# Turning the attention matrix of a two-layer graph network: from TensorE to VectorE blocks and DMAs

## The chip, the cores and the metric

The kernel runs on one core of a Trainium2 chip. The time is that of one execution on the device, in microseconds (us), from launch to end. Inputs lie in device memory.

## The reference, cut to what matters

64 graphs of 256 nodes with 512 features go through two layers. Each layer takes a normalised, rectified copy of x and adds its result to x.

```python
h = maximum(layernorm(x), 0)                    # layer 0: 4 heads of 64
q, k, v = heads(h @ Wq), heads(h @ Wk), heads(h @ Wv)
x = x + merge(softmax(where(adj, q k^T / 8, -max)) v) @ Wo + bo

h = maximum(layernorm(x), 0)                    # layer 1: 8 heads of 64
m = h @ map_w.T + map_b
cos = cosine(m, m) * ~adj                       # per head, 256 x 256
q, k = heads(m @ q_w.T + q_b), heads(m @ k_w.T + k_b)
p = softmax(where(adj, -1e10, q k^T / 8)) * keep
att = (cos > 0.1) * p                           # per head, 256 x 256
x = x + relu((att @ (h @ gcn_map_w.T + b)) @ gcn_W.T / (sum(att) + 1))
```

## The kernel before

One graph is one round. A round is software-pipelined: it runs the attention of layer 1 for graph a beside everything of graph n = a + 1 up to the layer-1 projections. There is a first round with no layer-1 attention, 62 rounds in a hardware loop, one more, and a last round with the attention of the last graph alone. The order of the work of each engine is written out by hand in five lists (L50 to L80: TENSOR, SCALAR, VECTOR, POOL, SYNC); each engine walks its own list strictly in order, and semaphores join them. A name in quotes (`"qk0"`, `"vv0"`) is a step of graph n, a pair (`("cos", 2)`) one of graph a for the head pair 2 of 0 to 3. Where two steps of one engine stand in the list, the second never starts before the first.

Layer-1 attention, for each pair p of heads a and b:

- `score` (L800, helper L767): TensorE makes q k^T into two PSUM banks, one for each head; VectorE (`score_a`, `score_b`, L607) masks it into the SBUF tile `att` and finds the row's extreme; ScalarE (`exp_a`, `exp_b`, L475) takes the exponential in place.
- `cos` (L804): TensorE makes the cosines into two more banks; VectorE (`cos_a`, `cos_b`, L618) compares them with 0.1 and multiplies `att` in place.
- `turn_a`, `turn_b` (L808, helper L743): TensorE transposes `att` of one head, four blocks of 128 x 128, into the head's score bank, and ScalarE (L481) copies it to the SBUF tile `uT`. There is one `uT`, with room for one pair.
- `value` (L812, helper L779): TensorE multiplies v by `uT` (8 matmul records of 256 columns for the pair); ScalarE copies the result (L485), `back` on TensorE turns it (L817), on VectorE scales it (L634), on GpSimd adds it to `x_res` (L410).

`att` has two buffers, used by pairs alternately. Of layer 0 and the projections, `ht` are transposes of h, `qk`, `m`, `q`, `k`, `v0`, `vv`, `wo` are projections (L755, L763), `s` scores, `pt` transposes of the probabilities, `av` their product with v, `ss`, `rt`, `bc` the norms for the cosines. In the TENSOR list `value` 3 is followed by `vv0`, `ss`, all `q` and `k` projections and `vv1` of graph n, and only then comes `score` 0 of the next round.

The DMAs of the loop are issued by SyncE (its queue is SP in the profile), four for each graph: the next x, the result, a copy of `x_mid` to `x_res`, the next adjacency matrix. Each names all 128 partitions.

Of the kernel before, what the change touches and what calls it, by code (L numbers as in the profile page):

```python
# [18 lines left out]
COS_THRESHOLD = 0.1  # L19
MASKED_L1 = -1e10  # L20
# [3 lines left out]
def gnn_two_layers(nc, x, adj, wq, wk, wv, wo, bo, map_t, map_b, q_t, q_b, k_t, k_b, gcn_map, gcn_map_b, gcn_t, out):  # L24
# [26 lines left out]
        "ht0a", ("score", 0), "ht0b", ("cos", 0), "qk0", "qk1", ("turn_a", 0), "qk2", ("turn_b", 0), "s0", "s1", ("value", 0),  # L51
        "qk3", ("back", 0), ("score", 1), ("cos", 1), "s2", "s3", "pt0", "v0", "pt1", ("turn_a", 1), ("turn_b", 1), "pt2",
        "pt3", ("value", 1), "av", ("back", 1), ("score", 2), ("cos", 2), "wo0", "wo1", ("turn_a", 2), ("turn_b", 2),
        ("value", 2), ("score", 3), ("back", 2), "ht1a", "ht1b", ("cos", 3), "m0", "m1", "m2", ("turn_a", 3), ("turn_b", 3),
# [17 lines left out]
    ]  # L72
    POOL = [
        ("unit", 0), "mid", "mask0", "sum0", "sum1", ("unit", 1), ("back", 0), "sum2", "sum3", "rstd1", ("back", 1),
        ("back", 2), "m0", "rstd0", "m1", "m2", "m3", "pow", "mask1", ("back", 3)
    ]
# [5 lines left out]
    bank_of = {s: 4 + k % PBANKS for k, s in enumerate(PRODUCTS)}  # L82
# [21 lines left out]
    with ctx:  # L104
# [40 lines left out]
        att = sb("att", [128, 2, 2, C, N])  # L145
# [5 lines left out]
        gcn_rows = att[:, :, :, :, :].rearrange("p a b c n -> p (a b c n)").rearrange("p (h d) -> p h d", d=D)  # L151
# [77 lines left out]
        gram_full = count("gram_full")  # L229
        gated = count("gated")  # L230
        t_full = count("t_full")
        uT_ready = count("uT_ready")
        uv_full = count("uv_full")
        oT1_ready = count("oT1_ready")
        o_full = count("o_full")
# [692 lines left out]
```

## Time and profile before

| | |
|---|---|
| runs | 4121.55 us median of 3 (4118.8 to 4130.23) |
| the profiled execution | 4121.26 us, span 4119.5 us |
| mean granted TensorE clock | 0.993 |
| TensorE busy | 3931.4 us, 95% |
| VectorE busy | 2608.3 us, 63% |
| ScalarE busy | 1979.3 us, 48% |
| GpSimd busy | 1324.3 us, 32% |

The page gives the busy time of each engine, then the span in 40 slices with tenths of busy time in each. The slices are even from the second to the last but one: the rounds are alike, so one round of the timeline stands for all. A matmul's recorded time holds its latency, and neighbours overlap; what one costs in a dense stream is read from start to start.

### The profile page before, as it was taken

To read this page: it belongs to the slowest core of one execution; us is meant where nothing else is said; L and a number is where in the kernel's file an instruction comes from. 1 tells how busy PE (TensorE), PEld (TensorE's weight loads), DVE (VectorE), ACT (ScalarE), POOL (GpSimd) and SP (SyncE) were. 2 spreads that over 40 slices of the span, in tenths; PEclk is the share of its full clock that TensorE was granted. 3 is DMA by queue.
4 is the path that set the end of the run, shared out by engine and by line. 5 is a ranking of instruction groups with operands and counts; after the bars stand their busy time and mean duration, and the time that the engine had idled before them with its cause. 6 is when DMAs were issued, how large, how long until landed. Compare 5 with 4: busy or idle time off the path is not lost.

```text
span 4119.5 us, 105002 instructions
## 1 busy us (share of the span) xinstructions
PE 3931.4 (95%) x32976; PEld 3437.0 (83%) x32976; DVE 2608.3 (63%) x9426; ACT 1979.3 (48%) x5583; POOL 1324.3 (32%) x2007
## 2 busy tenths in 40 slices
PE   7999999999999999999999999999999999999997
PEld 6888888888888888888888888888888888888886
DVE  4666666666666666666666666666666666666664
ACT  3554544544545445445454454454454544544544
POOL 3333333333332333333333333333333333333332
PEclk8999999999999999999999999999999999999998
DMA  3000000000000000000000000000000000000000
GB/s 87 16 32 26 22 32 16 32 32 16 32 27 21 32 18 30 32 16 32 29 18 32 22 25 32 16 32 32 16 32 27 21 32 16 32 32 16 32 27 17
DMA packets 65544, 111.77 MB, mean 27 GB/s; under 512 B 20880, under 2 KB 22448, under 8 KB 65520
## 3 DMA queue, kind: packets, MB, share of 16 engines
q1 hardware_dynamic: 64928, 110.12, 7.8%
q0 software_dynamic: 592, 1.35, 0.2%
q8 instruction: 13, 0.21, 0.0%
q14 instruction: 11, 0.09, 0.0%
HBM read 44.34 MB, written 33.55 MB: 19 GB/s over the span
## 4 chain that ended last, share of the span: by engine, by line
PE 65%; DVE 12%; issue 11%; ACT 6%; POOL 4%; DVEq 1%; DMA 1%; POOLq 0%; ACTq 0%; SPq 0%
PE bank L755 34%; PE bank L763 9%; PE bank L748 7%; PE bank L783 6%; PE bank L775 4%; ACT prob L501 3%; PE bank L883 3%; POOL prob L417 2%; DVE x_mid L663 2%; ACT att L475 2%; DVE prob L650 2%; DVE att L607 2%; DVE att L618 1%; POOL rstd L362 1%; DVE hT L640 1%
## 5 line engine op out<-in xcount | busy, mean ns | idle before, releaser
L475 ACT ACTIVATE att<-att,nmax 128x256 f32<-128x256 f32 x1024 | 509.7, 500 | 299.6 <-DVE nmax L607 299.6
L417 POOL TENSOR_SCALAR prob<-prob,rsum 128x256 f32<-128x256 f32 x512 | 241.1, 487 | 631.2 <-DVE rsum L657 628.2
L755 PE MATMUL bank<-hT,w_qkv 128*128 128x256 f32 x3072 | 414.9, 288 | 4.7 <-DVE hT L640 4.7
L755 PE MATMUL bank<-qkm,w_k 128*128 128x256 f32 x3072 | 416.6, 285 | 0.0
L755 PEld LDWEIGHTS bank<-hT,w_qkv 128*128 128x128 f32 x3072 | 376.9, 189 | 37.9 <-issue 24.2
L755 PE MATMUL bank<-hT,w_map 128*128 128x256 f32 x3072 | 396.7, 285 | 5.1 <-DVE hT L640 1.0
L618 DVE SCALAR_TENSOR_TENSOR att<-bank,att 128x256 f32<-128x256 f32 x1024 | 392.3, 420 | 4.0
L755 PE MATMUL bank<-qkm,w_q 128*128 128x256 f32 x3072 | 390.8, 283 | 0.0
L755 PEld LDWEIGHTS bank<-hT,w_map 128*128 128x128 f32 x3072 | 372.5, 189 | 18.4 <-DVE hT L640 17.3
L763 PE MATMUL bank<-w_v,hT 128*128 128x512 f32 x1536 | 385.3, 399 | 0.0
L755 PEld LDWEIGHTS bank<-qkm,w_k 128*128 128x128 f32 x3072 | 380.1, 188 | 5.0
L481 ACT ACTIVATE uT<-bank 128x512 f32<-128x512 f32 x512 | 292.2, 598 | 181.1 <-PE bank L748 169.5
L515 ACT ACTIVATE q<-bank,bias_q 128x256 fp32r<-128x256 f32 x256 | 121.0, 473 | 537.1 <-PE bank L755 535.2
L607 DVE CUSTOM_DVE_ANT_0 att<-bank,mask 128x256 f32<-128x256 f32 x1024 | 372.1, 420 | 7.3 <-PE bank L775 2.3
L755 PEld LDWEIGHTS bank<-qkm,w_q 128*128 128x128 f32 x3072 | 373.4, 189 | 0.1
L763 PEld LDWEIGHTS bank<-w_v,hT 128*128 128x128 f32 x1536 | 278.6, 188 | 82.6 <-issue 24.2
L783 PE MATMUL bank<-uT,v 128*64 128x256 f32 x2048 | 280.1, 395 | 49.4 <-ACT uT L481 49.4
L410 POOL TENSOR_TENSOR x_res<-x_res,rel 128x256 f32<-128x256 f32 x256 | 189.0, 738 | 420.4 <-DVE rel L634 420.4
L689 DVE SCALAR_TENSOR_TENSOR q<-bank,bias_q,q 128x256 fp32r<-128x256 f32 x256 | 117.1, 478 | 321.4 <-ACT q L515 321.4
L359 POOL TENSOR_SCALAR var_e<-mv 128x2 f32<-128x2 f32 x128 | 24.7, 193 | 913.9 <-DVE mv L540 913.9
L634 DVE SCALAR_TENSOR_TENSOR rel<-bank,fac 128x256 f32<-128x256 f32 x256 | 108.7, 424 | 314.6 <-PE bank L820 310.1
L515 ACT ACTIVATE k<-bank,bias_k 128x256 fp32r<-128x256 f32 x256 | 121.5, 474 | 373.9 <-PE bank L755 373.9
(122 smaller groups left out, 7949.6 us busy)
## 6 DMA issues: line engine op xcount, KB each, us to landing
x_in<-x SPq DMA_DIRECT2D x64, 512.0 KB, 3.4
x_res<-x_mid SPq DMA_DIRECT2D x64, 512.0 KB, 3.1
out<-x_res SPq DMA_DIRECT2D x64, 512.0 KB, 2.8
adj<-adj SPq DMA_DIRECT2D x64, 64.0 KB, 2.6
att<-gcn_map POOLq DMA_DIRECT2D x2, 512.0 KB, 9.0
x_mid<-wq SPq DMA_DIRECT2D x1, 512.0 KB, 5.6
x_res<-wk SPq DMA_DIRECT2D x1, 512.0 KB, 6.8
v<-wv SPq DMA_DIRECT2D x1, 512.0 KB, 7.7
```

What stands on the lines that cost most here:

```text
L410: g.tensor_tensor(part, part, rel[:, :, :], ALU.add).then_inc(res_added, 1)
L417: last = g.tensor_scalar(prob0[:, hd, c, :], prob0[:, hd, c, :], rsum0[:, hd, c:c + 1], 0.0, ALU.mult, ALU.add)
L475: s_.activation(e_sl, e_sl, ACT.Exp, bias=nmax1[:, p, c, e:e + 1], scale=-1.0, accum_out=esum1[:, p, c, e:e + 1]).then_inc(exp1_done, 1)
L481: s_.activation(uT[:, e, :], t_bank[e][:, :], ACT.Copy).then_inc(uT_ready, 1)
L515: s_.activation(dst[:, 0, t, :], bank[bank_of[kind]][:, 0:N], ACT.Identity, bias=bias[:, t:t + 1]).then_inc(high_done, 1)
L607: v_.tensor_tensor_reduce(out=att[:, p % 2, e, c, :], in0=score_bank[e][:, c * N:c * N + N], in1=mask1[:, c, :], scale=-SCALE, scalar=FLT_ ...
L618: v_.scalar_tensor_tensor(e_sl, gram_bank[e][:, c * N:c * N + N], COS_THRESHOLD, e_sl, ALU.is_gt, ALU.mult, accum_out=usum1[:, p, c, e:e + ...
L748: last = t_.transpose(dst[:, b * 128:b * 128 + 128], src_of(outer, c), ident[:, :])
L755: last = t_.matmul(dst, w(ws, k)[:, t * 128:t * 128 + 128], rhs[:, rs, k, :], start=(k == 0 and i == 0), stop=(k == KT - 1 and i == 2))
L763: last = t_.matmul(dst, lhs[:, ls, k, c * 128:c * 128 + 128], w(ws, k), start=(k == 0 and i == 0), stop=(k == chunks - 1 and i == 2))
L775: last[e] = t_.matmul(banks[e][:, c * N:c * N + N], left[r, ls, c * 128:c * 128 + 128], right[r, rs, :], start=(i == 0), stop=(i == 2))
L783: last = t_.matmul(dst[64 * e:64 * e + 64, :], v[:, jc, (hd0 + e) * DH:(hd0 + e + 1) * DH], rhs(e, jc), start=(jc == 0), stop=(jc == C - 1))
```

## The change

- `turn_a` and `turn_b` go from TensorE and from ScalarE. VectorE gets `flip_a` and `flip_b` instead: one instruction for each head transposes every 32 x 32 block of `att` (128 partitions x 512 elements) in place.
- SyncE gets a step `("shift", p)` for each pair: it waits until `value` of the pair before is done (`uv_full`, since `uT` still has one buffer), and then, for each head, waits for the head's flip and issues 16 DMAs. Each carries 32 partitions x 128 elements (512 bytes a partition, 16 KB in all) from `att` to `uT`, so that the blocks come to lie where the whole transpose has them. `value` p waits for all 32 DMAs of its pair.
- The tile `att` is laid out in blocks. `score` and `cos` on TensorE read their right side and write PSUM in pieces of 32 elements; `value` reads `uT` so; the mask of layer 1 is made in that order too.
- `value` and `back` share PSUM bank 4; the other products of graph n have three banks in place of four. `score` and `cos` wait for VectorE's reads of their banks.
- All five lists are put in a new order.

```diff
     TENSOR = [
...
+        ("score", 0), "ht0a", "ht0b", ("cos", 0), ("score", 1), "qk0", "qk1", "qk2", "qk3", "s0", "s1", ("cos", 1),
+        ("score", 2), "s2", "s3", ("value", 0), "v0", "pt0", "pt1", ("back", 0), "pt2", "pt3", ("cos", 2), "av", ("value", 1),
+        ("score", 3), "wo0", "wo1", ("back", 1), ("cos", 3), ("value", 2), "ht1a", "ht1b", ("back", 2), "m0", "m1", "m2", "m3",
+        ("value", 3), "vv0", "ss", ("back", 3), "q0", "k0", "q3", "rt", "k3", "q2", "bc0", "q1", "k1", "k2", "vv1", "bc1"
     ]
     SCALAR = [
...
+        ("unit", 0), "ht0a", "ht0b", ("exp_a", 0), ("exp_b", 0), "qk0", "qk1", ("unit", 1), ("exp_a", 1), "qk2", "qk3",
+        ("exp_b", 1), "exp0", "exp1", ("value", 0), "exp2", "exp3", "pt0", "pt1", "pt2", "pt3", ("exp_a", 2), ("exp_b", 2),
+        "av", ("exp_a", 3), ("exp_b", 3), ("value", 1), ("value", 2), "ht1a", "ht1b", "m0", "m1", "m2", "m3", ("value", 3),
+        "q0", "k0", "q3", "k3", "q2", "q1", "k2", "k1"
     ]
     VECTOR = [
...
+        ("score_a", 0), ("score_b", 0), "ht0a", "ht0b", ("cos_a", 0), ("flip_a", 0), ("cos_b", 0), "qk0", ("flip_b", 0),
+        ("score_a", 1), "qk1", "qk2", ("score_b", 1), ("factor", 0), "qk3", "s0", ("cos_a", 1), "s1", "sum0", "s2", "s3",
+        ("flip_a", 1), "sum1", ("cos_b", 1), "sum2", ("flip_b", 1), "sum3", "v0", ("back", 0), ("factor", 1), ("score_a", 2),
+        ("score_b", 2), ("cos_a", 2), ("cos_b", 2), ("flip_a", 2), ("factor", 2), "av", ("flip_b", 2), ("score_a", 3),
+        ("score_b", 3), "wo0", "wo1", ("back", 1), ("cos_a", 3), "norm1", ("flip_a", 3), ("cos_b", 3), "ht1a", "ht1b",
+        ("flip_b", 3), "m0", "m1", ("back", 2), ("factor", 3), "stats0", "m2", "m3", "vv0", ("back", 3), "ss", "norm0", "q0",
+        "k0", "q3", "rt", "k3", "q2", "bc0", "q1", "k1", "k2", "vv1", "bc1"
     ]
     POOL = [
...
+        "mask0", ("unit", 0), "mid", ("unit", 1), "sum0", "sum1", "sum2", "sum3", ("back", 0), "rstd1", ("back", 1), "m0",
+        "m1", ("back", 2), "mask1", "rstd0", "m2", "m3", "pow", ("back", 3)
     ]
-    PBANKS = 4
+    PBANKS = 3
     SYNC = [
-        "x", ("out", 0), "move", "adj"
+        ("shift", 0), ("shift", 1), ("shift", 2), "x", ("shift", 3), ("out", 0), "adj", "move"
     ]
...
-        att = sb("att", [128, 2, 2, C, N])
+        att = sb("att", [128, 2, 4, 2, C, C, 32])
...
+                    elif kind == "shift":
+
+                        sp.wait_ge(uv_full, pairs(a, p))
+                        sp.sem_inc(passed_sync, 1)
+                        for e in range(2):
+                            sp.wait_ge(flipped, pairs(a, p, 2) + e + 1)
+                            sp.sem_inc(passed_sync, 1)
+                            for rows in range(4):
+                                for cols in range(4):
+                                    sp.dma_start(uT_blocks[32 * cols:32 * cols + 32, rows, e, :, :, :].rearrange("p c j f -> p (c j f)"),
+                                                 att[32 * rows:32 * rows + 32, p % 2, cols, e, :, :, :].rearrange("p c j f -> p (c j f)")).then_inc(turned[p], 16)
...
-                    elif kind in ("turn_a", "turn_b"):
-                        e = "ab".index(kind[5])
-                        act.wait_ge(t_full, pairs(a, p, 2) + e + 1)
-                        act.wait_ge(uv_full, pairs(a, p))
-                        s_.activation(uT[:, e, :], t_bank[e][:, :], ACT.Copy).then_inc(uT_ready, 1)
...
+                        if e == 0:
+                            dve.wait_ge(turned[(p + 2) % 4], BLOCK_MOVES * (a + (1 if p < 2 else 2)))
+                            dve.sem_inc(passed_vector, 1)
...
+                    elif kind in ("flip_a", "flip_b"):
+
+                        e = "ab".index(kind[5])
+                        dve.wait_ge(gated, pairs(a, p, 4) + 2 * e + 2)
+                        dve.sem_inc(passed_vector, 1)
+                        blocks = att[:, p % 2, :, e, :, :, :].rearrange("p b c j f -> p b (c j f)")
+                        v_.transpose(blocks, blocks).then_inc(flipped, 1)
...
+                    elif kind == "value":
+                        pe.wait_ge(turned[p], BLOCK_MOVES * (a + 2))
                         pe.wait_ge(rel_done, pairs(a, p))
-                    elif kind in ("turn_a", "turn_b"):
-                        e = "ab".index(kind[5])
-                        pe.wait_ge(gated, pairs(a, p, 4) + 2 * e + 2)
-                        transposes(t_bank[e], lambda jc, c: att[:, p % 2, e, c, jc * 128:jc * 128 + 128]).then_inc(t_full, 1)
```

## Rows read from the trace of the kernel before

**Rows 1.** Busy time of each engine in one round (--windows, steady state), clock and DMA last.

```profile
core 0: us, PE busy (x) PEld busy (x) DVE busy (x) ACT busy (x) POOL busy (x), PEclk, DMA share, GB/s
2000.00:2063.15 63.15, 60.91 (x516) 53.31 (x514) 40.53 (x147) 30.70 (x87) 20.52 (x31) 1.00 0.08 26
```

**Rows 2.** Waits of the whole span: who waited for whom, us in total, times, longest.

```profile
SPq L309 <- POOL x_res L410: 3414.3, 64, 62.2
```

**Rows 3.** Timeline of SyncE's queue: start, duration of the issue, in steady rounds.

```profile
2048.52 0.40 SPq L310 DMA_DIRECT2D out<-x_res  x1
2051.41 0.47 SPq L321 DMA_DIRECT2D x_res<-x_mid  x1
2111.69 0.40 SPq L310 DMA_DIRECT2D out<-x_res  x1
```

**Rows 4.** The same view at the kernel's start: DMAs issued back to back.

```profile
0.75 0.45 SPq L285 DMA_DIRECT2D x_in<-x  x1
1.26 0.45 SPq L286 DMA_DIRECT2D adj<-adj  x1
1.75 0.47 SPq L294 DMA_DIRECT2D x_mid<-wq  x1
2.27 0.51 SPq L294 DMA_DIRECT2D x_res<-wk  x1
2.81 0.51 SPq L294 DMA_DIRECT2D v<-wv  x1
```

**Rows 5.** Four lines' issues: count, ns min/median/max, first and last start us.

```profile
L305 SPq DMA_DIRECT2D x_in<-x x63: 368/387/397, 35.2 to 3952.0; - x63
L310 SPq DMA_DIRECT2D out<-x_res x64: 394/396/411, 154.0 to 4115.0; - x64
L321 SPq DMA_DIRECT2D x_res<-x_mid x64: 472/480/537, 56.4 to 4075.5; - x64
L326 SPq DMA_DIRECT2D adj<-adj x63: 373/392/400, 84.1 to 4009.7; - x63
```

**Rows 6.** From issue to landing, us: first of L321, then of L326.

```profile
DMA to landing us min/median/max: 2.9/3.1/3.1
...
DMA to landing us min/median/max: 1.8/2.6/4.3
```

**Rows 7.** Timeline of TensorE in one round: value 3 to score 0.

```profile
2032.91 1.08 PE L783 MATMUL bank<-uT,v 128*64 128x256 f32 x8
2033.92 3.06 PE L763 MATMUL bank<-w_v,hT 128*128 128x512 f32 x12
2053.80 0.60 PE L748 MATMUL bank<-ident,h 128*128 128x128 f32 x4
2054.33 0.97 PE L775 MATMUL bank<-k,q 64*128 64x256 f32 x12
```

**Rows 8.** Timelines: last cos_a 0 of that round; score 0, turn of the last round.

```profile
2058.88 0.42 DVE L618 SCALAR_TENSOR_TENSOR att<-bank,att 128x256 f32<-128x256 f32 x1
...
4077.93 0.98 PE L775 MATMUL bank<-k,q 64*128 64x256 f32 x12
4081.34 0.65 PE L748 MATMUL bank<-ident,att 128*128 128x128 f32 x4 [1.38 <-DVE att L618]
```

**Rows 9.** VectorE groups by line: busy us, mean ns of one, idle before.

```profile
L549 DVE CAST pick<-uT 128x512 fp32r<-128x512 f32 x1 | 0.4, 426 | 4.0 <-POOL uT L350 4.0
L546 DVE TENSOR_SCALAR h<-x_mid,mv,rstd 128x512 f32<-128x512 f32 x128 | 89.2, 736 | 84.3 <-POOL rstd L362 84.3
```

**Rows 10.** Windows while TensorE stands, and while it is busy again.

```profile
56.00:58.00 2.00, 0.00 (x0) 0.00 (x0) 1.24 (x4) 0.00 (x0) 0.29 (x2) 1.00 0.20 80
60.00:62.00 2.00, 1.68 (x8) 1.68 (x8) 0.26 (x1) 0.00 (x0) 0.00 (x0) 0.55 0.00 0
36.00:38.00 2.00, 2.00 (x14) 2.00 (x12) 1.19 (x7) 0.38 (x1) 0.00 (x0) 0.50 0.93 353
42.00:43.00 1.00, 1.00 (x6) 1.00 (x6) 0.00 (x0) 0.47 (x1) 0.00 (x0) 0.50 0.00 0
43.00:44.00 1.00, 1.00 (x9) 1.00 (x9) 0.00 (x0) 0.00 (x0) 0.00 (x0) 0.94 0.00 0
```

**Rows 11.** Timeline of TensorE in the last round: a value at the lower clock.

```profile
4101.00 1.97 PE L783 MATMUL bank<-uT,v 128*64 128x256 f32 x8 [0.69 <-ACT uT L481]
```

**Rows 12.** Timeline of TensorE: two turns of att and what follows.

```profile
2071.98 1.04 PE L748 MATMUL bank<-ident,att 128*128 128x128 f32 x8
2072.86 1.34 PE L748 MATMUL bank<-ident,prob 128*128 128x128 f32 x8
```

**Rows 13.** TensorE's wait for uT, in the waits; packets of SyncE's queue.

```profile
PE bank L783 <- ACT uT L481: 49.4, 67, 0.8
...
q1 hardware_dynamic: 64928, 110.12, 7.8%
```

More of the change, by code:

```diff
@@ L50, in gnn_two_layers @@
     TENSOR = [
[L51 to L54, printed above, removed]
@@ L75, in gnn_two_layers @@
-        ("back", 2), "m0", "rstd0", "m1", "m2", "m3", "pow", "mask1", ("back", 3)
+        "mask0", ("unit", 0), "mid", ("unit", 1), "sum0", "sum1", "sum2", "sum3", ("back", 0), "rstd1", ("back", 1), "m0",
+        "m1", ("back", 2), "mask1", "rstd0", "m2", "m3", "pow", ("back", 3)
     ]
-    PBANKS = 4
+    PBANKS = 3
     SYNC = [
-        "x", ("out", 0), "move", "adj"
+        ("shift", 0), ("shift", 1), ("shift", 2), "x", ("shift", 3), ("out", 0), "adj", "move"
     ]
     PRODUCTS = [s for s in TENSOR if isinstance(s, str)]
-    bank_of = {s: 4 + k % PBANKS for k, s in enumerate(PRODUCTS)}
+    bank_of = {s: 5 + k % PBANKS for k, s in enumerate(PRODUCTS)}
@@ L230, in gnn_two_layers @@
         gated = count("gated")
-        t_full = count("t_full")
-        uT_ready = count("uT_ready")
+        flipped = count("flipped")
+        turned = [count(f"turned{p}") for p in range(PAIRS1)]
         uv_full = count("uv_full")
@@ L286, in _ @@
                 sp.dma_start(adj8[:, :, :], adj[0].rearrange("(c p) j -> p c j", p=128)).then_inc(adj_loaded, 16)
+                for p in range(PAIRS1):
+                    sp.sem_inc(turned[p], BLOCK_MOVES)
                 for k, (src, _) in enumerate(PIECES):
@@ L430, in body @@
                             pool.sem_inc(passed_gpsimd, 1)
-                        g.tensor_scalar(mask1[:, :, :], adj8[:, :, :], MASKED_L1, 0.0, ALU.mult, ALU.add).then_inc(mask1_ready, 1)
+                        for c in range(C):
+                            g.tensor_scalar(mask1[:, c, :].rearrange("p (b j f) -> p b j f", j=C, f=32),
+                                            adj8[:, c, :].rearrange("p (j b f) -> p b j f", j=C, f=32), MASKED_L1, 0.0,
+                                            ALU.mult, ALU.add).then_inc(mask1_ready, 1)
                         for c in range(C):
@@ L601, in body @@
                             if p == 0:
[L602 to L605 removed]
+                                dve.wait_ge(mask1_ready, C * (a + 1))
+                        if e == 0:
+                            dve.wait_ge(turned[(p + 2) % 4], BLOCK_MOVES * (a + (1 if p < 2 else 2)))
+                            dve.sem_inc(passed_vector, 1)
                         for c in range(C):
[L607 removed]
+                            v_.tensor_tensor_reduce(out=att[:, p % 2, :, e, c, :, :].rearrange("p b j f -> p b (j f)"), in0=in_blocks(score_bank[e][:, c * N:c * N + N]), in1=in_blocks(mask1[:, c, :]),
                                                     scale=-SCALE, scalar=FLT_MAX, op0=ALU.add, op1=ALU.min,
@@ L765, in project_rows, with by_quarter, head_products @@
                 return last
-            def head_products(banks, left, right):
+            def by_quarter(ap, source):
+                return ap.rearrange("p (j b f) -> p b j f", j=C, f=32) if source else ap.rearrange("p (b j f) -> p b j f", j=C, f=32)
+            def head_products(banks, left, right, order=lambda ap, source: ap):
                 last = [None, None]
@@ L774, in head_products @@
                             r = slice(64 * e, 64 * e + 64)
-                            last[e] = t_.matmul(banks[e][:, c * N:c * N + N], left[r, ls, c * 128:c * 128 + 128], right[r, rs, :],
-                                                start=(i == 0), stop=(i == 2))
+                            last[e] = t_.matmul(order(banks[e][:, c * N:c * N + N], False), left[r, ls, c * 128:c * 128 + 128],
+                                                order(right[r, rs, :], True), start=(i == 0), stop=(i == 2))
                 return last
@@ L782, in values @@
                     for e in range(2):
-                        last = t_.matmul(dst[64 * e:64 * e + 64, :], v[:, jc, (hd0 + e) * DH:(hd0 + e + 1) * DH], rhs(e, jc),
+                        last = t_.matmul(dst[64 * e:64 * e + 64, :].rearrange("p (c r f) -> p c r f", c=C, f=32), v[:, jc, (hd0 + e) * DH:(hd0 + e + 1) * DH], rhs(e, jc),
                                          start=(jc == 0), stop=(jc == C - 1))
@@ L856, in body @@
                         for t in range(PAIRS0):
-                            last = values(full[:, t * N:t * N + N], v0, 2 * t, lambda e, jc: ptm[:, 2 * t + e, jc * N:jc * N + N])
+                            last = values(full[:, t * N:t * N + N], v0, 2 * t, lambda e, jc: ptm[:, 2 * t + e, jc * N:jc * N + N].rearrange("p (c r f) -> p c r f", c=C, f=32))
                         last.then_inc(product_full, 1)
```

45 lines of the change are left out of this document (16 added, 29 removed), and 3 rows, old and new, of the table VECTOR.

## The prediction

> **What bounds the kernel now.** I read the page's busy times first, then one round by windows, then the timelines of TensorE and of SyncE's queue. One round, from one result's store to the next, takes 2111.69 - 2048.52 = 63.2 us [rows 3]; 64 of them are the kernel. In a round TensorE is busy 60.9 us at the full clock, VectorE 40.5, ScalarE 30.7 [rows 1]. So TensorE's own stream is the round, and whatever leaves it would shorten it. SyncE's queue does next to nothing: it waits 3414 us of the span for the add that completes a result [rows 2], and issues four DMAs a round.
>
> **What leaves TensorE.** The turns of a pair take 2072.86 - 2071.98 = 0.88 us from start to start [rows 12], 3.5 us a round for four pairs. TensorE's wait for `uT`, 49.4 us in all, is 0.8 us a round [rows 13]. Were nothing late in their place, a round would take 63.2 - 4.3 = 58.9 us. ScalarE loses eight copies; it isn't the bound and this is worth nothing.
>
> **What is put in their place is a chain of its own.** `uT` has one buffer. The shift of pair p waits for `value` p-1, `value` p waits for the shift's 32 DMAs, and TensorE takes both in order. So from one `value` to the next there lie: the end of `value`, a hop to SyncE, 32 issues one after the other, the landing of the last, and nothing can overlap them but TensorE's other work. The question is what one issue costs.
>
> *One issue, T.* SyncE's rows show no 16 KB DMA, so I bound it. An issue takes the same for 64 KB (392 ns median, adjacency) as for 512 KB (387 ns, x) [rows 5]: its price doesn't follow the bytes, and I don't expect a small one to be cheaper. The cheapest of either is 368 ns; with the gap of 0.04 to 0.06 us to the next issue [rows 4], T is at least 0.42. The only copy from SBUF to SBUF, which these are, takes 480 ns [rows 5]: 0.53 with the gap. DMAs issued back to back start 0.49 to 0.54 us apart [rows 4], though none of them is from SBUF; with the 0.09 that SBUF to SBUF takes more, 0.63 is the upper end. I take 0.53, where two rows meet, and keep 0.42 and 0.63.
>
> The Trainium skill's page "DMA: Bandwidth & Descriptors", in its section on why a DMA increments its semaphore by 16, gives 512 sequencer cycles for a copy instruction on chips before the accelerated path; at the 1.2 GHz that "Trainium Kernel Development and Optimization" (NeuronCore Architecture) gives SyncE that is an estimate of 0.43 us. The rows' 0.37 to 0.51 lie about it; by it the round would come out near my cheap end.
>
> *Landing, L, from the last issue's start.* 2.6 us median for 64 KB, as little as 1.8; 3.1 for 512 KB from SBUF to SBUF [rows 6]. I take 2.4, nearer to the smaller transfer, with 1.8 and 3.1 as ends.
>
> *Hop.* The add into `x_res` ends 0.2 us before the store is issued; I take 0.2 for semaphore hops, an estimate that 0.1 either way moves by 0.8 us in two hops a pair.
>
> *Value.* 1.08 us at the full clock [rows 7], 1.97 at half [rows 11].
>
> *The first shift's chain:* 31 x 0.53 + 2.4 + 0.2 = 19.0 us from flip a of pair 0 to `value` 0. Flip b comes some 2 us behind flip a, within the 16 x 0.53 = 8.5 us that head a's issues take, so it costs nothing; beginning with the first head saves just that.
>
> *From value to value:* 1.97 + 19.0 = 21.0 us, three times: 63.0. Beside it TensorE has only v0, four pt, back, cos and av (about 8 us), then score 3, two wo, cos 3 (about 8), then two ht1 and four m (about 8): it stands for over half the time. VectorE's and ScalarE's work for the next pair fits in the same 21 us, so its flips are not late. The wait of `score_a` 2 for pair 0's DMAs is passed already when `value` 0 has run.
>
> *From value 3 to flip a 0 of the next round.* This stretch has no shift to hide in or beside, as `value` 3 stands ahead of vv0, ss, all q and k and vv1, and score 0 behind them. The old round takes 2054.33 - 2032.91 = 21.4 us from `value` 3 to score 0, with ht0a (2054.33 - 2053.80 = 0.5) between, which now comes later: 20.9 [rows 7]. From score 0 to the end of cos_a is 5.0 us in the full round (2059.30 less 2054.33) [rows 7, 8] and 3.4 in the last, where no ht stands between [rows 8]; with both ht behind score 0, I take 4.2. The flip of 128 x 512 is bounded by VectorE's other instructions of that size, 0.43 to 0.74 [rows 9]; no row shows a transpose on it. I take the dearer: 0.7. Together 4.9, ends 3.8 and 5.7. Seven of the eight flips, some 5 us, lie beside SyncE's issues; VectorE at 46 us is far from a bound here.
>
> SyncE's other work lies in that stretch too: out, adj and move, with the wait for the store to land (2051.41 - 2048.52 = 2.9 us [rows 3]), are some 14 us behind `value` 3, before the flip at 26. The load of x stands between shift 2 and shift 3: 0.39 us [rows 5], and while `value` 2 is awaited, so nothing.
>
> *TensorE's clock.* It stands 10 to 12 us ahead of each `value`. After the stop at 56 us the clock was at 1.00 for a while and at 0.55 in the window from 60; with TensorE fully busy from 36 us on, it stayed 0.50 up to 43 us and was 0.94 in the next [rows 10]: 1.2 GHz for 8 us of work, then 2.4. I expect this behind every stop. It costs three values 0.9 each (2.7, the fourth is within the next term) and the stretch behind `value` 3 the half of 8 us, 4.0. The other work beside the shifts has room.
>
> *The sum.* 20.9 + 4.0 + 4.9 + 19.0 + 63.0 = 111.8 us a round. With 64 rounds: the first result is stored at 154 us in this trace and the last 4.5 us before the end [rows 5], so 91 us of start stand ahead of the first round; in the last one nothing is queued between `value` 3 and the store, which I estimate at 9.5 us less. 91 - 9.5 + 4.5 = 86; 64 x 111.8 + 86 = 7241, and 2 us around the span (4121.26 to 4119.5; the median is 4121.55, the same). **7240 us.** The start's own new order and the three PSUM banks I put at nothing: TensorE waits more than it works. If pieces of 32 elements slow matmuls, score 0 and four values show it: doubled, 0.9 + 4 x 1.1 = 5.3 us a round, 340 us, within the range.
>
> **The rivals.**
>
> *A. Issues at their cheap end.* T 0.42, L 1.8: shift chain 15.0, round 20.9 + 4.9 + 15.0 + 3 x 16.1 = 89.0 with the clock kept, 5,780 us; with it lost 95.7, 6,210. For it: 368 to 392 ns are most of the loop's rows. Against: the one SBUF to SBUF row.
>
> *B. T 0.53, and the clock holds.* 105.1 a round, 6,810 us. Stops of 4 us have left it at 1.00 [rows 10]; these are longer.
>
> *C. Issues at their dear end.* T 0.63, L 3.1: shift chain 22.8, round 24.9 + 5.7 + 22.8 + 3 x 24.8 = 127.7, 8,260 us.
>
> *D. Not slower: a small DMA is issued nearly for nothing, and the transfers set the shift.* SyncE's packets took 0.078 x 4119.5 x 16 / 64,928 = 0.079 us each [rows 13]. A pair has 1,024, 64 on each engine: 5.1 us. Then the shift chain is 7.7, the round 20.9 + 4.9 + 7.7 + 3 x 8.8 = 59.9, just above TensorE's 58.9: 4121 - 63 x 3.3 = 3,910 us. It holds as long as 124T + 39.4 is under 63.2: T under 0.19. Against it stand all rows of the queue, the lowest at 0.37. The time from 0.19 to 0.42 would be slower already.
>
> The Trainium skill speaks for D: "DMA: Bandwidth & Descriptors", section "Issuing engines are not separate DMA queues", says the sequencer's time to initiate a DMA is usually small beside the DMA. In the rows 0.4 of 3 us is small indeed; but here 32 of them are in series behind one wait and the landing is paid once, so I give that rule little.
>
> **How the numbers follow.** My forecast 45%, A 24%, B 10%, C 15%, D and all else that ends at or below today's time 6%. The range is 5,750 to 8,000: it takes in A and B and most of the way to C. About 0.3% is what a measurement of this kernel can tell from no change (12 us). Slower 0.94, same 0.01, faster 0.05.
>
> **What would show it.** In the changed kernel's timeline SyncE's queue has runs of 32 issues with starts 0.53 us apart, 128 a round; the waits put TensorE's `value` behind these DMAs, near 45 us a round; the page has TensorE under 60% busy and a mean clock well under 0.99. The round is 112 us from store to store. Wrong would be: issues under 0.2 us apart (D); `value` waiting for anything else; or starts at 0.53 us and a round far from 105 to 112, which would mean that the chain isn't serial as the code reads.

## The result, and the profile after

The changed kernel takes 7836.5 us (median of 4 runs, 7835.3 to 7838.4) where the kernel before takes 4121.9: a ratio of 1.901, 95% interval 1.897 to 1.904. It is slower, by 3715 us. The forecast was 7240 us, with a range of 5750 to 8000.

The page of the changed kernel: busy time of the engines, the granted clock by slices (tenths of full speed), and the chain that ended last by line.

```profile
span 7834.8 us, 109125 instructions
...
PE 4256.1 (54%) x30928; PEld 3595.7 (46%) x30928; DVE 2998.1 (38%) x9938; ACT 1722.7 (22%) x5071; POOL 1352.6 (17%) x2071
...
PEclk7777777777777777777777777777777777777776
...
SPq L321 59%; PE bank L777 9%; PE bank L809 7%; DMA uT<-att 6%; PE bank L785 6%; PE bank L906 1%; PE bank L770 1%; PE bank L801 1%; DVE hT L663 1%; DVE att L642 1%; DVE att L634 1%; DVE att L623 0%; PE bank L918 0%; PE bank L843 0%; SPq L317 0%
```

Before, the chain that ended last lay 65% on TensorE; now 59% of it is L321, SyncE issuing the moves from `att` to `uT`. No engine is busy for more than 54% of the span.

One round, store to store, by windows; it answers to [rows 1].

```profile
3958.51:4079.18 120.67, 65.69 (x484) 55.59 (x483) 46.55 (x155) 26.69 (x79) 20.97 (x32) 0.76 0.11 31
```

120.7 us in place of 63.2. TensorE is busy for 65.7 us of it, where it was 60.9, with a mean granted clock of 0.76; what is new is 55 us in which it stands. This round is a little shorter than most: from the first store to the last (201.5 to 7831.7 us, 63 steps) the mean is 121.1. SyncE's queue in the same stretch, which answers to [rows 3]:

```profile
3974.18 67.72 SPq L321 DMA_DIRECT2D uT<-att  x96
4042.36 0.40 SPq L311 DMA_DIRECT2D x_in<-x  x1
4045.35 20.21 SPq L321 DMA_DIRECT2D uT<-att  x32
4079.18 0.41 SPq L327 DMA_DIRECT2D out<-x_res  x1
4082.22 0.54 SPq L338 DMA_DIRECT2D x_res<-x_mid  x1
4094.85 35.19 SPq L321 DMA_DIRECT2D uT<-att  x50
```

32 issues of a pair last 20.2 us; the 96 of three pairs, with the two waits between them, 67.7. TensorE's side, its timeline at values 2 and 3 (last column: idle before, and who ended it):

```profile
4043.13 1.97 PE L809 MATMUL bank<-uT,v 128*64 128x256 f32 x8 [14.69 <-DMA uT<-att]
...
4066.83 1.98 PE L809 MATMUL bank<-uT,v 128*64 128x256 f32 x8 [13.31 <-DMA uT<-att]
```

From value 2 to value 3 it is 23.7 us: 1.97 of value and 0.25 to the first issue (4045.35), 19.6 to the last issue, 1.8 to its landing. `value` waits for the DMAs 256 times, once a pair and graph, 3518 us in all:

```profile
PE bank L809 <- DMA uT<-att: 3518.3, 256, 20.8
```

And the line of the moves and the flips, in ns min/median/max and by form (busy us, mean ns):

```profile
L321 SPq DMA_DIRECT2D uT<-att x8192: 507/590/1357, 95.4 to 7825.4; - x200
...
DMA to landing us min/median/max: 1.7/1.8/3.0
...
L642 DVE STREAM_TRANSPOSE att<-att 128x512 f32<-128x512 f32 x512 | 361.0, 705 | 10.7 <-DVE att L634 9.6
```

### The profile page after: what moved, and what is told of

Same layout as the page of the kernel before. It is cut to its first block, busy times and chain, and to the rows that moved or that the text cites. A ratio compares the mean times of both kernels' runs of the same rounds, so it can differ in the third digit from the quotient of the medians.

```text
span 7834.8 us, 109125 instructions
## 1 busy us (share of the span) xinstructions
PE 4256.1 (54%) x30928; PEld 3595.7 (46%) x30928; DVE 2998.1 (38%) x9938; ACT 1722.7 (22%) x5071; POOL 1352.6 (17%) x2071
## 3 DMA queue, kind: packets, MB, share of 16 engines
q0 software_dynamic: 592, 1.35, 0.1%
## 4 chain that ended last, share of the span: by engine, by line
SPq 60%; PE 26%; DMA 6%; issue 6%; DVE 3%; DVEq 0%; POOL 0%; ACT 0%; POOLq 0%; ACTq 0%
SPq L321 59%; PE bank L777 9%; PE bank L809 7%; DMA uT<-att 6%; PE bank L785 6%; PE bank L906 1%; PE bank L770 1%; PE bank L801 1%; DVE hT L663 1%; DVE att L642 1%; DVE att L634 1%; DVE att L623 0%; PE bank L918 0%; PE bank L843 0%; SPq L317 0%
## 5 line engine op out<-in xcount | busy, mean ns | idle before, releaser
L809 PE MATMUL bank<-uT,v 128*64 128x256 f32 x2048 | 505.4, 647 | 3518.3 <-DMA uT<-att 3518.3
L809 PEld LDWEIGHTS bank<-uT,v 128*64 128x64 f32 x2048 | 196.3, 217 | 3684.3 <-DMA uT<-att 3587.0
L499 ACT ACTIVATE oT<-bank 128x256 f32<-128x256 f32 x256 | 97.4, 380 | 3115.9 <-PE bank L809 3115.9
L663 DVE SCALAR_TENSOR_TENSOR hT<-bank,hT 128x512 fp32r<-128x512 f32 x256 | 167.9, 686 | 887.2 <-ACT hT L503 871.8
L708 DVE TENSOR_TENSOR v<-bank,bias_v 128x512 f32<-128x512 f32 x128 | 88.6, 692 | 1085.8 <-PE bank L785 1085.8
L785 PE MATMUL bank<-w_v,hT 128*128 128x512 f32 x1536 | 460.3, 457 | 0.0
L461 POOL TENSOR_TENSOR rn<-ssq,minus_half 128x16 f32<-128x16 f32 x64 | 200.4, 3131 | 1136.3 <-DVE ssq L715 1136.3
L785 PEld LDWEIGHTS bank<-w_v,hT 128*128 128x128 f32 x1536 | 335.8, 227 | 123.4 <-issue 47.7
L680 DVE RECIPROCAL rsum<-esum 128x2 f32<-128x2 f32 x256 | 39.4, 154 | 919.5 <-ACT prob L515 919.2
L441 POOL TENSOR_TENSOR ptm<-ptm 128x256 f32<-128x256 f32 x256 | 154.9, 617 | 1330.8 <-DVE qkm L694 1330.8
```

Of the source, the lines that this page charges most:

```text
L441: g.tensor_tensor(msq[:, t, :], m32[:, t, :], m32[:, t, :], ALU.mult).then_inc(msq_done, 1)
L461: g.tensor_tensor(rn[:, :], ssq[:, :], minus_half[:, :], ALU.pow).then_inc(rn_done, 1)
L499: s_.activation(oT1[:, :], v_bank[0][:, 0:N], ACT.Copy).then_inc(oT1_ready, 1)
L663: v_.scalar_tensor_tensor(flat(hT[:, 1, t:t + 2, :]), full[:, :], 0.0, flat(hT[:, 0, t:t + 2, :]).bitcast(F32), ALU.max, ALU.subtract).the ...
L785: last = t_.matmul(dst, lhs[:, ls, k, c * 128:c * 128 + 128], w(ws, k), start=(k == 0 and i == 0), stop=(k == chunks - 1 and i == 2))
L809: last = t_.matmul(dst[64 * e:64 * e + 64, :].rearrange("p (c r f) -> p c r f", c=C, f=32), v[:, jc, (hd0 + e) * DH:(hd0 + e + 1) * DH], r ...
```

## The experiments

The theory behind the forecast: the loss is a serial chain, 32 issues and one landing for each pair, between two values that share one `uT`. The rivals are that the landings, the bytes, the new order or the clock make it. Numbers 2 to 7 and 9 are single runs; where a time is said to change there, it changes by over 3%, and the runs of one kernel here differ by 0.3%.

**1. One DMA for each head.** The rest of the change stays, so this is what the change costs without its moves.

```diff
-                            for rows in range(4):
-                                for cols in range(4):
+                            for rows in range(1):
+                                for cols in range(1):
```

> One DMA for each head in place of 16; the other 15 are left out, so most of uT is not written. Theory (the 32 issues in series between two values are the loss, 0.65 us each as the changed kernel's trace has them): a chain shrinks by 30 issues, 19.5 us, and TensorE's own stream is the round again, 59 to 61 us, 3,830 to 3,950 us in all, faster than before. Rival 1 (the new order, the three banks, the block layout and the flips cost much by themselves): a round over 63.2 us, 4,150 us or more. Rival 2 (the landing of a DMA, not its issue, is the loss): hardly less than 7,800 us.

4001.3 us (3999.2 to 4002.3), ratio to before 0.970 (0.969 to 0.972): faster than the kernel before. A round, from one adjacency load to the next (2046.11 to 2107.87), is 61.8 us. TensorE's three largest waits:

```profile
PE bank L770 <- DVE h L561: 77.2, 64, 8.3
PE bank L809 <- DVE rel L657: 54.0, 63, 0.9
PE bank L785 <- DVE oT L682: 30.7, 63, 0.5
```

No wait for a DMA is among them. So 30 issues a pair are worth 3835 us, with the clock's fall in the waits for them, and what is left of the change (turns gone, order, banks, blocks, flips) is a gain of 3%. It lies outside the 3,830 to 3,950 us that I expected: a round gains 1.4 us and not the 4.3 that I had counted for TensorE's turns and its wait for `uT`. All waits of TensorE but that for `uT` are 123 us in the kernel before and 224 here, 1.6 us a round more, and the mean clock is 0.977 in place of 0.993. Here the clock falls behind two stops, ahead of `value` 2 and ahead of `ht1a`, with 1.1 us of work between them, as the 1.87 us of the second row show. The kernel before has stops of 0.74 and 1.35 us in the same stretch, with 2.4 us of work between them, and its clock holds (third and fourth rows):

```profile
2084.94 1.08 PE L809 MATMUL bank<-uT,v 128*64 128x256 f32 x8 [0.84 <-DVE rel L657]
2087.11 1.87 PE L770 MATMUL bank<-ident,h 128*128 128x128 f32 x8 [1.09 <-DVE h L561]
...
2083.55 1.08 PE L783 MATMUL bank<-uT,v 128*64 128x256 f32 x8 [0.74 <-ACT uT L481]
...
2087.26 1.09 PE L748 MATMUL bank<-ident,h 128*128 128x128 f32 x8 [1.35 <-DVE h L546]
```

Score and value take 0.98 and 1.08 us at the full clock, as before: reading in pieces of 32 elements costs TensorE nothing that shows.

**2. The same DMAs with half the bytes.** 256 bytes a partition; half of `uT` isn't written.

```diff
-uT_blocks[32 * cols:32 * cols + 32, rows, e, :, :, :] ... att[..., cols, e, :, :, :]
+uT_blocks[32 * cols:32 * cols + 32, rows, e, 0:1, :, :] ... att[..., cols, e, 0:1, :, :]
```

> All 32 DMAs of a pair, each with 256 bytes a partition in place of 512; half of uT is not written. Theory (an issue's price doesn't follow the bytes): starts stay 0.65 us apart, 7,800 us. Rival (the queue is held up by what the DMA engines still have to move, which is why 0.65 stands where 0.53 was forecast): starts at 0.53 us or less, 120.7 - 124 x 0.12 = 106 us a round, 6,870 us or less.

7836.1 us, no change, and the same duration of an issue:

```profile
L321 SPq DMA_DIRECT2D uT<-att x8192: 507/590/1272, 95.1 to 7824.8; - x200
```

From 512 to 256 bytes a partition, bytes play no part, neither in the issue nor in a queue of work behind it.

**3. One DMA for both heads.** 16 for a pair, 1024 bytes a partition, after flip b.

```diff
-                        for e in range(2):
-                            sp.wait_ge(flipped, pairs(a, p, 2) + e + 1)
+                        sp.wait_ge(flipped, pairs(a, p, 2) + 2)
...
-att[32 * rows:32 * rows + 32, p % 2, cols, e, :, :, :]
+att[32 * rows:32 * rows + 32, p % 2, cols, :, :, :, :]
```

> The two heads of a pair go in one DMA: 16 for a pair with 1024 bytes a partition, begun when both heads are flipped; nothing is left out. Theory (price by the count of issues): value to value falls from 23.7 by 16 x 0.65 = 10.4 to 13.3 us, the round from 120.7 by 41.6 to 79 us plus some 2 us for waiting for flip b of pair 0, 81 us, 5,270 us. Rival (price by bytes): 7,800 us.

5751.5 us. The count sets the price: 16 issues are 10.0 us. But a round is 88.8 us (2030.39 to 2119.14 between two stores), not 81. The timelines of SyncE and TensorE:

```profile
2094.28 10.03 SPq L320 DMA_DIRECT2D uT<-att  x16
...
2088.32 1.98 PE L808 MATMUL bank<-uT,v 128*64 128x256 f32 x8 [4.72 <-DMA uT<-att]
2105.63 1.97 PE L808 MATMUL bank<-uT,v 128*64 128x256 f32 x8 [6.18 <-DMA uT<-att]
```

Value 2 is over at 2090.3, the shift of pair 3 begins at 2094.3, as flip b comes only then. With 32 issues there was room for it; with 16 the flips are the late ones at two of the three shifts behind a value, which my expectation had only for pair 0.

**4. Two issuing engines.** Head b's 16 DMAs are ScalarE's, four at a time between its other steps.

```diff
+                    elif kind[:5] == "shift":
+                        rows = int(kind[5])
+                        if rows == 0:
+                            act.wait_ge(uv_full, pairs(a, p))
+                            act.wait_ge(flipped, pairs(a, p, 2) + 2)
+                        for cols in range(4):
+                            act.dma_start(uT_blocks[..., rows, 1, ...], att[..., cols, 1, ...]).then_inc(turned[p], 16)
```

> Head a's 16 DMAs issued by SyncE, head b's 16 by ScalarE, in four groups between its other steps; nothing is left out. Theory (each issuing engine pays its own 0.65 us): value to value falls by up to 10.4 us, to 14 to 16 us as ScalarE has other steps between, the round to 80 to 90 us, 5,200 to 5,850 us. Rival (both queues share what generates the descriptors): starts twice as far apart while both issue, 7,500 us or more.

6185.5 us, a round of 95.6: a gain, and less than expected. Each engine pays its own price, hardly more beside the other's:

```profile
L322 SPq DMA_DIRECT2D uT<-att x4096: 507/592/1524, 93.6 to 6173.9; - x196
...
L503 ACTq DMA_DIRECT2D uT<-att x4096: 513/612/1811, 95.2 to 6174.2; - x196
```

The rival of a shared generator falls. What is short of the expectation is no longer the DMAs alone: TensorE waits 573 us for them, but 372 and 182 us for ScalarE's copies (`oT`, `ptm`), which now stand behind its issues, and 395 and 210 us for VectorE. One pair's ScalarE issues ran from 2025.7 to 2036.1 us, and its value at 2040.8, 19.0 us behind the value before it in place of 14 to 16, waited for no DMA: TensorE had stood 2.9 us for ScalarE's copy of `ptm` just ahead of `av`.

**5. TensorE kept busy in its waits.**

```diff
+                        pe.wait_ge(rel_done, pairs(a, p))
+                        for _ in range(100):
+                            t_.matmul(bank[4][:, N:2 * N], w_k[:, 0, 0, 0:128], w_k[:, 0, 1, 0:N], start=True, stop=True)
                         pe.wait_ge(turned[p], BLOCK_MOVES * (a + 2))
-                        pe.wait_ge(rel_done, pairs(a, p))
```

> TensorE is given 100 matmuls of 256 columns (12 us at the full clock) ahead of each value, into the unused half of bank 4, whose result nobody reads, in the time in which it waits for the DMAs. Theory (the clock's fall is a term of its own: the values behind a stop at half the clock, and the first work behind each): value takes 1.08 in place of 1.97 us, the stretch behind value 3 is some 4 us shorter, the round 120.7 - 6.7 = 114 us, 7,410 us in all, at a mean clock near 1. Rival (TensorE's clock is hidden by the chain, as the chain waits for nothing of TensorE but value): 7,830 less 64 x 0.9 x 4, 7,600 us; or, if the matmuls run longer than the wait, above 7,830 us.

7583.6 us, mean clock 0.972 in place of 0.752: 253 us less, 4.0 a round. The direction is right and the size nearer to the rival. Timelines of TensorE and SyncE:

```profile
2048.24 12.14 PE L837 MATMUL bank<-w_k 128*128 128x256 f32 x100
2061.36 1.08 PE L809 MATMUL bank<-uT,v 128*64 128x256 f32 x8 [0.98 <-DMA uT<-att]
...
2087.83 32.35 SPq L321 DMA_DIRECT2D uT<-att  x47
```

Value is back at 1.08 us (three of them count, 2.7; the fourth lies in the stretch behind value 3), and from value 3 to the next shift it is 26.5 us, where the changed kernel has 4094.85 - 4066.83 = 28.0: 1.5 and not 4.0. In the changed kernel the clock behind value 3 is back sooner than [rows 10] had it:

```profile
4069.00:4070.00 1.00, 1.00 (x3) 0.81 (x4) 0.00 (x0) 0.24 (x1) 0.00 (x0) 0.50 0.00 0
4070.00:4071.00 1.00, 1.00 (x5) 0.77 (x5) 0.00 (x0) 0.00 (x0) 0.00 (x0) 0.90 0.00 0
```

A mean of 0.90 in the second window puts the return at about 4070.2, 3.4 us behind the start of value 3; what half the clock cost in that time is half of it, 1.7.

**6. The price of an issue by itself.** The kernel before, with six groups of eight DMAs on SyncE's idle queue in each round.

```diff
+                    elif kind == "probe":
+                        for i in range(8):
+                            sp.dma_start(probe[32 * (i % 4):32 * (i % 4) + 32, ...], bias_v[...]).then_inc(probed, 16)
+                        sp.wait_ge(probed, 768 * a + 128)
...
```

> The kernel before with a step on SyncE's idle queue in each round: six groups of eight DMAs into a tile that nothing reads, each group waited for: 32 partitions x 512 bytes from SBUF; the same with 128 bytes; with 1024 bytes; 128 partitions x 256 bytes from SBUF; 32 partitions x 512 bytes from device memory; 16 partitions x 512 bytes from SBUF. Theory (SBUF to SBUF and back to back each add to an issue, bytes and partitions don't): 0.65 us apart for every group from SBUF, 0.05 to 0.1 less from device memory. Rival (the price follows the descriptors): 16 partitions half of 32, 128 partitions four times. The time stays within 1% of 4,120 us, as the queue has 57 us idle a round and nothing waits for it but the store of the result, or rises where that store comes late.

4124.3 us, unchanged. The six groups by line: 32 partitions x 512 bytes; x 128; x 1024; 128 partitions x 256 bytes; from device memory; 16 partitions x 512 bytes.

```profile
L312 SPq DMA_DIRECT2D probe<-bias_v x512: 521/590/995, 101.3 to 4082.7; - x171
L316 SPq DMA_DIRECT2D probe<-bias_v x512: 507/591/1425, 107.6 to 4088.9; - x171
L320 SPq DMA_DIRECT2D probe<-bias_v x512: 507/591/1319, 114.6 to 4095.1; - x171
L324 SPq DMA_DIRECT2D probe<-bias_v x512: 465/602/678, 120.9 to 4104.3; - x171
L328 SPq DMA_DIRECT2D probe<-wq x512: 331/421/1326, 127.4 to 4109.4; - x171
L332 SPq DMA_DIRECT2D probe<-bias_v x512: 561/589/818, 132.3 to 4115.5; - x171
```

From SBUF to SBUF an issue is 0.59 to 0.60 us whatever its bytes and its partitions; from device memory 0.42. The rival by descriptors falls. Eight from SBUF last 4.94 us, so their starts are (4.94 - 0.59) / 7 = 0.62 us apart; the pair's 32 are (20.21 - 0.59) / 31 = 0.63. Eight from device memory last 3.60 us, 0.45 apart. That back to back costs something too shows where the trace of the changed kernel is cut to the beginning of the shift at 4045.35: the first issue takes 0.52 us, the ones behind it 0.59, with 0.04 of gap.

**7. Two buffers for `uT`.** A shift waits for the value two pairs before. For the room the two masks are in bfloat16.

```diff
+        uT_odd = sb("uT_odd", [128, 2, C * N])
...
-                        sp.wait_ge(uv_full, pairs(a, p))
+                        sp.wait_ge(uv_full, pairs(a, p) - 1)
```

> uT has two buffers, by pair, and a shift waits for value of the pair two before it; for the room both masks are in bfloat16 (with 3e38 for the largest float). All 32 DMAs of a pair stay. Theory (the chain is issue, landing, hop and value in series; with two buffers the issues of four pairs run on one after the other, and landing, hop and value fall out three times; what stays in series is the 26 us from value 3 to the next flip a): 26 + 4 x 20.8 + 2 = 111 us a round, 7,230 us. Rival 1 (the queue alone is the bound): 128 x 0.65 + 2 = 85 us, 5,550 us. Rival 2 (no change, as the single buffer isn't what holds the shifts): 7,830 us.

7290.4 us, a round of 112.6 (1997.76 to 2110.39 between two stores). SyncE's queue:

```profile
1997.76 0.41 SPq L328 DMA_DIRECT2D out<-x_res  x1
...
2013.44 20.23 SPq L322 DMA_DIRECT2D uT<-att  x32
2034.06 20.21 SPq L322 DMA_DIRECT2D uT_odd<-att  x32
2054.58 20.18 SPq L322 DMA_DIRECT2D uT<-att  x32
...
2075.94 20.21 SPq L322 DMA_DIRECT2D uT_odd<-att  x32
```

The shifts run on with 0.3 to 0.4 us between them, 1.2 at the last, where the load of x stands; the round is 1.6 us over the 111 expected. The single buffer costs 8 us a round of the 57 lost. The four shifts take 83 of the 112.6, and the stretch behind value 3 still stands in series with them.

**8. Value one stage later.** 16 DMAs a pair (as 3), two buffers (as 7), and new lists in which value p stands behind work that hides the moves. Nothing is left out.

```diff
-        ("score", 2), "s2", "s3", ("value", 0), "v0", "pt0", "pt1", ("back", 0), "pt2", "pt3", ("cos", 2), "av", ("value", 1),
...
+        "s1", ("cos", 1), "s2", ("score", 2), "s3", "v0", "pt0", "pt1", "pt2", "pt3",
+        ("cos", 2), "av", ("value", 0), ("score", 3), "wo0", "wo1", ("back", 0), ("cos", 3), ("value", 1), "ht1a",
+        "ht1b", ("back", 1), "m0", "m1", "m2", "m3", ("value", 2), ("back", 2), "q0", "ss",
...
```

> The whole computation: 16 DMAs for a pair with 1024 bytes a partition, uT in two buffers, masks in bfloat16, and all five lists in another order, in which value p stands one stage later (value 0 behind av, value 1 behind wo, value 2 behind m, value 3 among the q and k projections, ahead of vv0). Theory (the DMAs cost only while TensorE waits for them; a pair now takes 15 x 0.63 + 1.8 = 11.3 us from flip b to value, and SyncE's 64 issues 41 us of a round): TensorE's own stream is the round, as it was with one DMA for each head, 61 to 62.5 us, 3,950 to 4,040 us, 2 to 4% faster than before. Rival (issues that run beside other DMAs, or the flips' and the waits' places, still hold value up): over 63.2 us a round, above 4,120 us.

4162.6 us, ratio 1.010 (1.008 to 1.011): slower than the kernel before by 1.0%. TensorE waits for DMAs 30.5 us in all, but once a round for VectorE's `back` 0 (143.4 us), with the clock falling behind it:

```profile
2032.47 1.08 PE L813 MATMUL bank<-uT_odd,v 128*64 128x256 f32 x8 [2.16 <-DVE rel L661]
...
2032.00:2040.00 8.00, 7.02 (x45) 6.11 (x46) 6.34 (x19) 3.87 (x13) 1.05 (x2) 0.79 0.34 109
```

The moves are nearly hidden, and the theory failed all the same: TensorE's own stream is not the round. The rival has the number right, and of its two causes the one that shows is a wait's place; a delay by DMAs beside other DMAs does not.

**9. The same without the new order.** Against number 8:

```diff
-        "s1", ("cos", 1), "s2", ("score", 2), "s3", "v0", "pt0", "pt1", "pt2", "pt3",
-        ("cos", 2), "av", ("value", 0), ("score", 3), "wo0", "wo1", ("back", 0), ("cos", 3), ("value", 1), "ht1a", ...
+        ("score", 2), "s2", "s3", ("value", 0), "v0", "pt0", "pt1", ("back", 0), "pt2", "pt3", ("cos", 2), "av", ("value", 1),
+        ("score", 3), "wo0", "wo1", ("back", 1), ("cos", 3), ("value", 2), "ht1a", "ht1b", ("back", 2), ...
```

> The same 16 DMAs for a pair, the same two buffers and masks, in the order of the changed kernel. Theory: what is left of the chain is flip b to value 11.3 us a pair, in part beside the issues of the next; value p stands ahead of the work that could hide it, and the scores of pair 2 stand behind back 0 on VectorE, so values alternate with waits: 79 to 86 us a round, 5,150 to 5,600 us. Rival (count and buffer alone are enough, the order is not the point): 62 to 66 us, 4,000 to 4,300 us.

5498.3 us, as expected; TensorE waits 1220 us for DMAs, against 30.5 in number 8. Against number 3 the second buffer gives 253 us. Count and buffer alone don't do it; value has to stand where the moves are done.

**10. Another order**, meant to have no stop over 0.8 us. Against number 8:

```diff
-        ("cos", 2), "av", ("value", 0), ("score", 3), "wo0", "wo1", ("back", 0), ("cos", 3), ("value", 1), "ht1a", ...
+        "av", ("cos", 2), ("value", 0), "wo0", "wo1", ("score", 3), "ht1a", "ht1b", ("cos", 3), ("back", 0),
+        "m0", "m1", "m2", "m3", ("value", 1), ("back", 1), "q0", "k0", "q3", "ss",
+        "k3", "q2", ("value", 2), "rt", "q1", "bc0", ("back", 2), "k1", "k2", ("value", 3), ...
```

> The whole computation, as with value one stage later (16 DMAs a pair, two buffers, bfloat16 masks), in an order in which no wait of TensorE is to be longer than 0.8 us; the last order had one of 2.2 us ahead of value 1, for back 0 on VectorE, and the clock's mean in the 8 us behind it was 0.79. Theory (that stop and the clock's fall behind it were what stood between 63.7 us and the 61.8 of one DMA for each head): 61.5 to 62.5 us a round, 4,020 to 4,080 us. Rival (it is the DMAs beside the other work after all): no better than 4,150 us.

4239.3 us, ratio 1.028 (1.027 to 1.029): worse, and above the 4,150 us of the rival too. In making the order I had left out TensorE's waits ahead of `score` and `cos`, and one of 3.3 us came in:

```profile
2060.49 1.65 PE L805 MATMUL bank<-k,q 64*128 64x256 f32 x12 [3.33 <-DVE nmax L627]
```

Behind it TensorE runs at half the clock again (the mean is 0.50 from 2062 to 2066 us, and the scores take 1.65 in place of 0.98). That this order had no stop over 0.8 us was wrong. The rival's cause, the DMAs beside other work, is not in the waits, 20 us for DMAs in all; whether DMAs slow other work was tested for the next order alone.

**11. A third order, with those waits counted.**

```diff
+        ("cos", 2), "av", ("score", 3), "wo0", "wo1", ("value", 0), ("back", 0), ("cos", 3), ("value", 1), "ht1a",
+        "ht1b", ("back", 1), "m0", "m1", "m2", "m3", ("value", 2), "q0", "ss", "k0",
+        "q3", "k3", "rt", ("back", 2), "q2", "q1", ("value", 3), "bc0", "k1", ("back", 3),
```

> The whole computation as before (16 DMAs a pair of 1024 bytes a partition, two buffers, bfloat16 masks), in a third order: value 0 behind wo, value 1 behind cos 3, value 2 behind m, value 3 among the q and k projections. The first such order had one stop of TensorE of 2.2 us a round, the second one of 3.3 us (ahead of score 3, behind VectorE's work on wo), and the clock fell behind both; here no wait is to be over 1.5 us. Theory (stops of TensorE by order, and the clock behind them, are what is left; the DMAs are hidden): 60.5 to 62.5 us a round, 3,960 to 4,080 us, faster than before. Rival (the way through VectorE and DMAs can't be hidden whole, whatever the order): 4,120 us or more.

4037.6 us (4035.5 to 4038.4), ratio to before 0.979 (0.978 to 0.981), mean clock 0.991: faster than the kernel before by 2.1%, and than the changed one by far. SyncE's queue and the values:

```profile
2010.61 10.05 SPq L325 DMA_DIRECT2D uT<-att  x16
2021.11 10.03 SPq L325 DMA_DIRECT2D uT_odd<-att  x16
2031.62 10.02 SPq L325 DMA_DIRECT2D uT<-att  x16
...
2042.80 10.03 SPq L325 DMA_DIRECT2D uT_odd<-att  x16
...
2029.38 1.08 PE L813 MATMUL bank<-uT,v 128*64 128x256 f32 x8
2032.46 1.08 PE L813 MATMUL bank<-uT_odd,v 128*64 128x256 f32 x8 [0.15 <-DMA uT_odd<-att]
2042.93 1.08 PE L813 MATMUL bank<-uT,v 128*64 128x256 f32 x8 [0.59 <-DMA uT<-att]
2054.93 1.08 PE L813 MATMUL bank<-uT_odd,v 128*64 128x256 f32 x8
```

The last issue of each shift is over 1.3 to 8.7 us ahead of its value (2020.66 to 2029.38, 2031.14 to 2032.46, 2041.64 to 2042.93, 2052.83 to 2054.93); what TensorE still waits for DMAs is 0.15 and 0.59 us. Its longest stop in the round is 1.0 us.

All waits of TensorE in the three orders are 332, 371 and 272 us (numbers 8, 10 and 11), with mean clocks of 0.966, 0.943 and 0.991. Number 8 waits 60 us more than number 11 and takes 127 more in its profiled span, number 10 waits 100 more and takes 197 more: about twice the wait. That the other half is the clock agrees with the clocks; no run keeps the clock up in those two orders.

**12. That order with one DMA a pair**, the other 15 left out.

```diff
-                        for rows in range(4):
-                            for cols in range(4):
+                        for rows in range(1):
+                            for cols in range(1):
```

> The same third order with one DMA for each pair in place of 16 (the other 15 left out, the second buffer set to zero at the start). Theory (16 DMAs a pair are hidden wholly): within 0.3% of the kernel with all of them. Rival (they delay value, or contend with the engines for SBUF): 1% or more below it.

4020.7 us, ratio to before 0.975 (0.974 to 0.977): 17 us or 0.4% below number 11, a little over the bound of the theory and well under the rival's 1%. The 0.7 us of waits in the fence above would be 47 us, were each passed on in full. The same comparison was expected to come out alike in the order of number 10; it has no time. With one DMA a pair this order is 20 us slower than the changed kernel's own with two (4001.3, number 1): by itself it isn't the better order, it is the one that has room for the moves.

## Why the prediction was right, point by point

- *The mechanism* was right: TensorE's `value` waits for the DMAs in each pair, and the moves are issued one after the other between two values. Shown by 1 (without the issues the loss is gone), 2 (the bytes don't matter) and 3 (half the count). What puts them in the round is above all where `value` stands (8 and 11 against 9, with 16 DMAs a pair); the single buffer by itself is 8 us a round (7).
- *T* was mis-sized, 0.633 for 0.53. I had two rows agree on 0.53 that each lacked one part: the copy from SBUF stood alone, the ones back to back came from device memory. Both parts together were my dear end, which is what it measured. 31 x 0.103 is 3.2 us a shift, 12.8 a round.
- *Landing* 1.8 for 2.4, -2.4 a round: it was the low end of [rows 6], where I had gone toward the median of a transfer four times as large.
- *From value 3 to flip a* 28.0 for 29.8. Over half of the clock's term there was too much, 1.5 to 1.7 measured for 4.0: [rows 10] come from the start, another pattern of work than this. The values at half the clock were right, 1.97. TensorE stood 12 to 15 us ahead of each value, not 10 to 12, and 55 us a round, not 45.
- *The flip* 0.705 for 0.7. The other seven lie beside the issues as put; with half the issues two of them came late (3).
- The sum: 111.8 + 12.8 - 2.4 - 1.8 = 120.4, measured 120.7 in this round and 121.1 on the mean; in all 7836 for 7240. Of these 596 us T is the cause, and the range held it by luck: with T at 0.633 and all else as I had it, the time would have been 7240 + 64 x 12.8 = 8059, above 8,000. Two smaller errors the other way brought it back. What came is rival C's T with rival A's landing.
- *B* rested on a wrong reading: the clock was at 1.00 while TensorE stood, from 56 us on, but in the window in which it took up work again it was 0.55 [rows 10]. Those rows show a clock that falls behind a stop of 4.8 us, not one that holds.
- *D*, the rival on the other side, failed where I put it, at the price of an issue. Its floor of 58.9 us would not have been reached either: with 30 of 32 issues gone a round was 61.8.
- The Trainium skill's "DMA: Bandwidth & Descriptors", section "Issuing engines are not separate DMA queues", says that initiating a DMA is usually little beside the DMA. Here one issue is 0.59 us beside a landing of 1.8, and the 32 in series are 20.2 us beside one landing: in such a series the rule doesn't hold.
- The 512 cycles for a copy instruction of the same page of the Trainium skill, section "Why a DMA increments its semaphore by 16 and not by 1", are an estimate of 0.43 us at SyncE's 1.2 GHz (the Trainium skill's "Trainium Kernel Development and Optimization", NeuronCore Architecture). That agrees with the 0.42 from device memory and not with the 0.59 from SBUF.

What stays open: whether the kernel before, with TensorE's turns, would gain as much from lists sought in the same way; it wasn't tried. So the 2% of number 11 belongs to moves, buffers, masks and order together. Nor is it known what makes an issue from SBUF dearer by 0.17 us than one from device memory, or why an issue behind another takes 0.07 more than the first.

## What to carry to other kernels

Count the DMAs of a step, not their bytes, and multiply by the spacing of issues back to back of the same kind of source; if that product lies between a producer and a consumer and there is no other work to fill the wait, it is added to the round, and a second buffer alone gives little back (8 us of 57). Work that leaves the busiest engine pays only when what comes in its place is started early enough and awaited late: the moves cost 3835 us in the changed kernel and 17 us in number 11, each against the same kernel without most of them, and with the count and the buffer but not the place of number 11, the kernel was still 1376 us behind the one before (number 9). Stops of TensorE can cost more than their length, as the clock can fall behind them, so an order is to be judged by its stops and not by its sum of work alone. The longest stop doesn't decide it: in the kernel before the clock held behind stops of 0.74 and 1.35 us with 2.4 us of work between them, and in number 1 it fell behind 0.84 and 1.09 us with 1.1 us between.

## What the hardware showed that I had not expected

- An issue on SyncE's queue, behind another, takes 0.59 to 0.60 us from SBUF to SBUF, the same for 128 to 1024 bytes a partition and for 16 to 128 partitions, and 0.42 us from device memory to SBUF (32 partitions x 512 bytes). The first of a pair's row takes 0.52.
- SyncE and ScalarE issued side by side at 0.59 and 0.61 us each (number 4): the second queue is a second rate.
- Stops of TensorE of 2.2 us (number 8) and 3.3 us (number 10) were each followed by a stretch at half the clock; in number 11, with no stop over 1.0 us a round, the mean granted clock was 0.991.
